# A gated linear-attention and experts kernel: score groups of a head taken by query halves with keys descending, and a new table of places

## What is computed

```python
scores = jnp.einsum('bthd,bshd->bhts', q, k) * scale
logdecay = jnp.where(mask[None, None], Gh[:, :, :, None] - Gh[:, :, None, :], -jnp.inf)
lamw = jnp.einsum('bthl,tsl->bhts', lam, lvl_oh)
A = scores * jnp.exp(logdecay) * lamw
y = jnp.einsum('bhts,bshd->bthd', A, v).reshape(b, t, H * HD)
out = y @ Wo.T + x                      # then a layer norm
...
x = x + _L0_attn_ref(_layernorm(x, axis=-1), ...)
x = x + _L0_ffn_ref(_layernorm(x, axis=-1), ...)
```

## Time and profile before

| | |
|---|---|
| median of 3 runs | 1608.45 us (1607.65 to 1608.62) |
| the profiled execution | 1608.22 us, its span 1606.1 us |
| PE busy | 1456.4 us (91%) |
| POOL busy | 1143.1 us (71%) |
| ACT busy | 1141.3 us (71%) |
| DVE busy | 1030.0 us (64%) |
| granted clock of PE, mean | 0.968 |

### The profile page before, as it was taken

How to read it: one execution, slowest core, us unless ns; L and a number is a source line. 1 busy time by engine, 2 the same in 40 slices (tenths; PEclk the granted TensorE clock), 3 DMA queues, 4 the chain that set the end, 5 groups by cost and what they waited for, 6 DMA issues and landing times.

```text
span 1606.1 us, 29807 instructions
## 1 busy us (share of the span) xinstructions
PE 1456.4 (91%) x10678; PEld 1210.6 (75%) x10678; DVE 1030.0 (64%) x2466; ACT 1141.3 (71%) x3299; POOL 1143.1 (71%) x1067
## 2 busy tenths in 40 slices
PE   5799997899989999899989999899998999989975
PEld 5588886778867887777877788678786887878853
DVE  5457565676657766586655866467674676647665
ACT  2689886786768767686766967678676886867631
POOL 1486779766896678956798667975679666896570
PEclk8799999999999999999999999999999999999987
DMA  5200100010100101001010010001010000100000
GB/s 176 64 18 16 39 28 15 10 37 20 36 15 7 38 22 36 13 15 42 10 35 13 25 36 20 23 16 35 23 36 12 10 26 19 36 16 28 8 8 13
DMA packets 80332, 44.01 MB, mean 27 GB/s; under 512 B 21832, under 2 KB 78522, under 8 KB 80058
## 3 DMA queue, kind: packets, MB, share of 16 engines
q1 hardware_dynamic: 79484, 41.83, 9.2%
q10 hardware_dynamic: 702, 0.29, 0.1%
HBM read 32.39 MB, written 9.18 MB: 26 GB/s over the span
## 4 chain that ended last, share of the span: by engine, by line
PE 55%; POOL 18%; DVE 12%; ACT 9%; issue 4%; DMA 1%; ACTq 0%; SPq 0%; POOLq 0%; DVEq 0%
PE o_ps L1320 15%; PE l_ps L1251 7%; PE s_ps L1235 6%; POOL a_lo L596 6%; PE s_ps L1237 6%; PE s_ps L1236 6%; PE aux L1235 4%; ACT w_all L714 4%; PE aux L1236 4%; PE aux L1237 4%; DVE a_all L912 2%; ACT a_hi L737 2%; POOL ra L581 2%; POOL e_rs L602 1%; POOL yx L441 1%
## 5 line engine op out<-in xcount | busy, mean ns | idle before, releaser
L596 POOL TENSOR_TENSOR a_lo<-a_all,a_hi 128x512 fp32r<-128x512 f32 (+2 forms) x640 | 709.1, 1125 | 323.9 <-ACT a_hi L737 322.7
L912 DVE TENSOR_TENSOR a_all<-s_ps,w_all 128x512 f32<-128x512 f32 (+3 forms) x768 | 422.6, 554 | 488.4 <-PE s_ps L1237 476.3
L714 ACT ACTIVATE w_all<-l_ps,bias 128x128 f32<-128x128 f32 x2304 | 628.5, 386 | 58.1 <-PE l_ps L1251 57.5
L737 ACT ACTIVATE a_hi<-a_all 128x512 fp32r<-128x512 f32 (+2 forms) x640 | 364.0, 591 | 254.8 <-DVE a_all L912 251.5
L1320 PE MATMUL o_ps<-a_hi,v_all 128*128 128x512 f32 (+2 forms) x1280 | 472.1, 373 | 56.9 <-POOL a_lo L596 56.8
L1320 PEld LDWEIGHTS o_ps<-a_hi,v_all 128*128 128x128 f32 x1280 | 243.9, 191 | 110.5 <-POOL a_lo L596 72.5
L1235 PE MATMUL s_ps<-q_hi,xt_hi 128*128 128x512 f32 (+3 forms) x768 | 290.4, 378 | 2.5 <-DVE a_all L912 2.5
L1236 PE MATMUL s_ps<-q_lo,xt_hi 128*128 128x512 f32 (+3 forms) x768 | 268.3, 349 | 0.0
L1237 PE MATMUL s_ps<-q_hi,xt_lo 128*128 128x512 f32 (+3 forms) x768 | 268.0, 349 | 0.0
L1320 PE MATMUL o_ps<-a_lo,v_all 128*128 128x512 f32 (+2 forms) x640 | 232.4, 363 | 0.0
L1237 PEld LDWEIGHTS s_ps<-q_hi,xt_lo 128*128 128x128 f32 x768 | 147.0, 191 | 17.1
...
## 6 DMA issues: line engine op xcount, KB each, us to landing
...
```

The costliest lines, as they stand in the source:

```text
L596: pool.tensor_tensor(a_lo[r][:, 0:t1 - t0], a[r][:, 0:t1 - t0], a_hi[r][:, 0:t1 - t0].bitcast(F32), ALU.subtract).then_inc(a_lo_done, 1)
L714: last = act.activation(w[k][:, W_AT[j] + dd, :].rearrange("p (f c) -> p f c", f=2), l_ps[:, :, slot * HF:(slot + 1) * HF], ACT.Exp, bias= ...
L737: act.activation(a_hi[r][:, 0:t1 - t0], a[r][:, 0:t1 - t0], ACT.Copy).then_inc(a_hi_done, 1)
L912: dve.tensor_tensor(a[(n * NG + g) % NA][:, 0:t1 - t0], s_ps[:, g % 2, 0:t1 - t0], w[n % 2][:, at:at + (t1 - t0) // P, :].rearrange("p i n ...
```

## The change

- GROUPS is ordered anew. First come the queries 0 to 512 with key tiles 3, 2, 1, 0 (widths 128, 256, 384, 512), then the queries 512 to 1024 with key tiles 7 to 0 (128, 256, 384 and five times 512). The FULL groups are now numbers 0 and 4.
- `weigh` waits at each group for the units that this group reads (UNITS_FOR: 1, 2, 3, 4, 1, 2, 3, 4, 5, 5, 5, 5) instead of for all five at group 0. `scores` waits for the second half of q at group 4 instead of at group 1, `values` for each value piece at the first group that reads it, and the value pieces are made in the order of tile pairs 1, 0, 3, 2.
- o_done and y_done become a semaphore for each half of the queries. The first half of o_ps is complete with group 3, the second with group 11. The residual of the second half stands at group 4.
- The tables of places are new. Among the moves: t_apply goes from POOL to ACT (places 56, 58, 64, 80), a quarter of apply2 too (place 101), xb(0) goes ahead of dev1 on POOL, T(0) on PE from place 92 to 104, `total` of the first half from place 273 to 285, the gate step 0 on DVE from place 145 to 144, and the expansions on POOL from places 10 and 21 of a head to 7 and 13.

```diff
--- before.py
+++ after.py
@@ -53,12 +53,8 @@
 
 BIAS_AT = [sum(NC - k for k in range(d)) for d in range(NC)]
 
-GROUPS = []
-for _j in range(NC):
-    for _lo in (0, T // 2):
-        _a = max(_j * P, _lo)
-        if _a < _lo + T // 2:
-            GROUPS.append((_j, _a, _lo + T // 2))
+KEY_ORDER = [(j, f) for f in range(2) for j in reversed(range(NC // 2 * (f + 1)))]
+GROUPS = [(j, max(j * P, f * T // 2), (f + 1) * T // 2) for j, f in KEY_ORDER]
 NG = len(GROUPS)
 
 UNITS = [[(0, 0, 8)], [(1, 1, 7)], [(2, 2, 6)], [(3, 3, 5), (5, 5, 3)], [(4, 4, 4)]]
@@ -151,12 +147,23 @@
 MEAN_VAR = 6
 
 
+V_ORDER = (1, 0, 3, 2)
 LAG = 4
 NA = LAG + 1
 Q_U, NV = 2, 4
 FULL = [g for g, (_j, _a, _b) in enumerate(GROUPS) if _b - _a == P]
 SPLIT = [g for g in range(NG) if g not in FULL]
 FULL_KEYS = [GROUPS[g][0] for g in FULL]
+
+FIRST_OF = [[_a // (T // 2) for _j, _a, _b in GROUPS].index(f) for f in range(2)]
+LAST_OF = [NG - 1 - [_a // (T // 2) for _j, _a, _b in reversed(GROUPS)].index(f) for f in range(2)]
+FIRST_KEYS = {[_j // 2 for _j, _a, _b in GROUPS].index(u): u for u in range(NC // 2)}
+UNIT_OF = {}
+for _u, _parts in enumerate(UNITS):
+    for _d, _i, _n in _parts:
+        for _dd in range(_d, NC if _d == 5 else _d + 1):
+            UNIT_OF[_dd] = _u
+UNITS_FOR = [1 + max(UNIT_OF[i - _j] for i in range(_a // P, _b // P)) for _j, _a, _b in GROUPS]
 
 SLOTS = H * NG
 HALF = T // 2
@@ -169,36 +176,35 @@
 U_AT = {0: 0, 3: 1, 5: 2, 7: 3, 10: 4}
 Q_AT = {6: 0, 20: 1}
 V_AT = {11: 0, 26: 1, 36: 2, 46: 3}
-Q_OUT = {11: 0, 21: 1}
-V_HIGH = {9: 0, 28: 1, 37: 2, 45: 3}
-V_LOW = {18: 0, 32: 1, 41: 2, 49: 3}
-EXPAND_A, EXPAND_B = 10, 21
+Q_OUT = {12: 0, 21: 1}
+V_HIGH = {9: 0, 25: 1, 37: 2, 45: 3}
+V_LOW = {14: 0, 31: 1, 41: 2, 51: 3}
+EXPAND_A, EXPAND_B = 7, 13
...
-             77: [('t_apply', 2)], 81: [('t_apply', 3)], 93: [('dev2', 0)], 96: [('apply2', 0)], 97: [('apply2', 1)],
+ACT_MORE = {12: [('y', 0)], 28: [('y', 1)], 56: [('t_apply', 1)], 58: [('t_apply', 0)], 64: [('t_apply', 2)],
+POOL_MORE = {29: [('xb', 0)], 32: [('dev1', 0)], 33: [('apply1', 0)], 40: [('apply1', 1)], 41: [('t_dev', 0)],
...
         q_hi_done, v_hi_done, v_full_done = sem("q_hi_done"), sem("v_hi_done"), sem("v_full_done")
-        o_done, y_done, ready = sem("o_done"), sem("y_done"), sem("ready")
+        o_done, y_done = ([sem(f"{n}{f}") for f in range(2)] for n in ("o_done", "y_done"))
...
-                    if 2 * u + 1 in FULL_KEYS:
-                        act.activation(v_full[:, r, FULL_KEYS.index(2 * u + 1), :],
+                    j = 2 * V_ORDER[u]
+                    if j + 1 in FULL_KEYS:
+                        act.activation(v_full[:, r, FULL_KEYS.index(j + 1), :],
                                        bank(piece)[:, 2 * P:4 * P].rearrange("p (e n) -> p e n", e=2),
...
@@ -906,8 +916,7 @@
                     at = W_AT[j] + t0 // P - j
                     if n == 0 and g == 0:
                         dve.wait_ge(s_n, 1)
-                    if g == 0:
-                        dve.wait_ge(w_done, (n + 1) * NU)
+                    dve.wait_ge(w_done, n * NU + UNITS_FOR[g])
                     dve.wait_ge(s_mm, n * NG + g + 1)
                     dve.tensor_tensor(a[(n * NG + g) % NA][:, 0:t1 - t0], s_ps[:, g % 2, 0:t1 - t0],
                                       w[n % 2][:, at:at + (t1 - t0) // P, :].rearrange("p i n -> p (i n)"),
@@ -915,11 +924,11 @@
 
                 def take_o(b, f):
 
-                    dve.wait_ge(o_done, 2 * b + f + 1)
+                    dve.wait_ge(o_done[f], b + 1)
                     if b:
                         dve.wait_ge(e["total"], 2 * (b - 1) + f + 1)
                     cols = slice(f * HALF, (f + 1) * HALF)
-                    dve.tensor_tensor(yt[:, cols], o_ps[:, cols], xt_hi[b % 2][:, cols].bitcast(F32), ALU.add).then_inc(y_done, 1)
+                    dve.tensor_tensor(yt[:, cols], o_ps[:, cols], xt_hi[b % 2][:, cols].bitcast(F32), ALU.add).then_inc(y_done[f], 1)
 
                 def statistics(src, stats, i0, s_st):
                     for i in range(i0, i0 + 2):
@@ -1116,8 +1125,10 @@
                             level_logs(b + 1, i)
                         if kind == "l_low" and b + 1 < B:
                             low_logs(b + 1, i)
-                        if kind == "o" and (b or i == 0):
-                            take_o(b - i, i)
+                        if kind == "o" and place >= 2 * NG * H:
+                            take_o(b, i)
+                        if kind == "o" and place < 2 * NG * H and b:
+                            take_o(b - 1, i)
                         if kind == "stat1" and b:
                             first_statistics(b - 1, 2 * i)
                         if kind == "mean1" and b:
@@ -1282,8 +1293,8 @@
                     k, b = n % 2, n // H
                     if n == 0 and g == 0:
                         pe.wait_ge(s_wetc, 2)
-                    if g < Q_U:
-                        wait_taken(pe, ("q", n, g))
+                    if g in FIRST_OF:
+                        wait_taken(pe, ("q", n, FIRST_OF.index(g)))
                     if n or g >= 2:
                         pe.wait_ge(a_done, n * NG + g - 1)
                     keys = slice(j * P, (j + 1) * P)
@@ -1304,11 +1315,10 @@
                     j, t0, t1 = GROUPS[g]
                     b, h = divmod(n, H)
                     r, vr = (n * NG + g) % NA, n % 3
-                    if h == 0 and g < 2:
-                        residual(b, g)
-                    if n % 2 == 0 and g == 0:
-                        for u in range(NV):
-                            wait_taken(pe, ("v", n // 2, u))
+                    if h == 0 and g in FIRST_OF:
+                        residual(b, FIRST_OF.index(g))
+                    if n % 2 == 0 and g in FIRST_KEYS:
+                        wait_taken(pe, ("v", n // 2, V_ORDER.index(FIRST_KEYS[g])))
                     o = o_ps[:, t0:t1]
                     if g in FULL:
                         pe.wait_ge(a_done, n * NG + g + 1)
@@ -1319,8 +1329,8 @@
                         for lhs, rhs in ((v_hi, a_hi), (v_hi, a_lo), (v_lo, a_hi)):
                             last = pe.matmul(o, lhs[:, vr, j, :], rhs[r][:, 0:t1 - t0],
                                              start=False, stop=True, skip_group_check=True)
-                    if h == H - 1 and g in FULL:
-                        last.then_inc(o_done, 1)
+                    if h == H - 1 and g in LAST_OF:
+                        last.then_inc(o_done[LAST_OF.index(g)], 1)
 
                 def claim(piece):
...
```

45 lines of the change are left out of this document (24 added, 21 removed), and 15 rows, old and new, of tables (DVE_MORE, PE_MORE).

## The result

The changed kernel takes 1598.04 us (median of 4 runs, 1596.55 to 1598.31), the kernel before beside it 1608.34 us (1607.65 to 1608.62). The ratio is 0.9935, with a 95% interval of 0.9917 to 0.9952. The change makes the kernel faster by 10.3 us, and not by the 34.5 of the forecast; the time lies 1 us outside the range.

A forecast was written before the change was run, and what follows sets the result against it. PE was taken as the bound, held up by POOL in about one and a half heads a batch. Main term 27.5 plus total 7.0 gave 34.5 us off 1608.22, so 1573.7 (1574 against the median); range 1560 to 1597.

The forecast's parts named there:

- What bounds the kernel: PE is the bound; POOL bounds about one and a half heads a batch, where PE idles 8.0 us.
- The main term: Heads 1 and 2: t_apply and a quarter of apply2 leave POOL, priced one to one at 27.5 us.
- The cap doesn't bind: Heads 1 and 2: the 4.44 us a batch taken off POOL is below PE's 8.0 us of idle time.
- Batch 7 as a trial: Batch 7, heads 1 and 2: POOL busy 5.3 us less, heads 5.7 us shorter, so the stretch follows POOL.
- The rule against ACT: Skill's advice of VectorE for add and mul; rows give it 1 us a batch on ACT; sum left unchanged.
- The group order: New sequence of groups in every head: 0, with bounds of 1.5 us either way for each of 7 batches.
- Gates: Head 3, a unit waiting 2.29 us for exps on ACT: counted 0, bounds 1 us either way a batch.
- total: Head 5: with total later on POOL, the values' 1.00 us wait goes in 7 batches, 7.0 us.
- Finer waits: PE's waits by units, halves and pieces: none of its waits in the rows is of that kind, so 0.
- the two ends: Start and end of the kernel, where the last group becomes 512 wide: counted 0, bounds -1 to +2 us.
- The lower clock: Head 1, PE clock 0.94: fewer gaps could give up to 1.8 us a batch, 1563 us; left out of the sum.
- part comes back: Rival, chance 0.30: POOL meets wide groups when behind, PE waits for a_lo at groups 9 to 11; 1582 to 1600 us.

The follow-up runs named there:

- x14: The changed kernel with level_ln at place 186 instead of 190 and apply1 moved from POOL to DVE at places 41 and 49: 1562.17 us, ratio 0.9702.
- x3: The kernel before with only t_apply and a quarter of apply2 moved from POOL to ACT: 1593.58 us, ratio 0.9905.
- x8: The changed kernel with t_apply and the last quarter of apply2 put back on POOL: 1614.59 us, ratio 1.0033.
- x5: The kernel before with t_apply and a quarter of apply2 on ACT and total of the first half at place 292: 1592.42 us, ratio 0.9896.
- x2: The kernel before, keeping its group order and coarse waits, with the changed kernel's tables of places: 1595.92 us, ratio 0.9921.
- x7: The changed kernel with level_ln on ACT at place 186 instead of 190: 1585.83 us, ratio 0.9850.
- x12: The kernel before, with its old group order and coarse waits, given all the new tables but level_ln at place 186: 1595.22 us, ratio 0.9918.

## Why the prediction was off, step by step

- *What bounds the kernel*: right. PE's waits for a_lo in head 1 were the place to win; x14 took most of them away (0.47 and 0.60 us are left in batch 2) and won 24 us more.
- *The main term*, the step that failed: 27.5 us forecast, 15.4 measured in the old order (x3) and 16.6 in the new (x8). "The cap doesn't bind" was wrong. It compared 4.44 us with all 8.0 us of idle time, but t_apply stands behind the first waits, and behind it there were 3.5 us, of which x3 won 2.8. The bound could be had from PE's timeline and the earlier trace rows: add up the idle time after 462.33. Batch 7 as a trial also misled, since there PE had 3.8 us less to do, which I noted and set aside, and since what POOL hadn't to do there included t_dev, which stands ahead of the waits.
- *The rule against ACT*: ACT took 0.516 us for a t_apply tile and had room; the move is the part that pays. Whether DVE would be better for t_apply wasn't tried; for apply1 DVE was good.
- *The group order*: put at 0 within 10 us. With the old places it costs 24 us, with the new ones between +2 and -9, by one entry of ACT's table. The bounds looked at widths and cover in one head and not at what a place number means once the widths change.
- *Gates and the tables of ACT*: "exp is earlier by 7 places and ln later by 3" spoke of the gates; level_ln, 4 places later, was not priced. This is the omitted step, 12 us: its two table loads had moved past a high_a that waits for DVE.
- *total*: 7.0 forecast, 3.7 measured alone, 1 to 2 in the new order, within the intervals. The named return of a bank's wait came.
- *Finer waits*, *the two ends*: 0, as forecast. From PE's first unit for the last head to the end the two kernels take 91.5 and 91.3 us.
- *The lower clock*: left out of the sum as a possible gain, and it became a small loss: in three of the seven batches head 1 stands at 0.88 and is 1.0 us longer than where it stands at 0.94 (last section). "I take batch 2 for all" hid that head 1 differed before too, from 1.00 in batch 1 to 0.89 in batches 5 and 6.
- *The rivals*: the range of "part comes back", 1582 to 1600, holds the result, and it had one part of the mechanism, PE's waits for a_lo. It put them at groups 9 to 11. One is there (group 11 of head 0, 0.79 us), but 3.9 us are at groups 1 and 2 of head 1. ACT's waits came too, at head 4, from level_ln and not from t_apply.

In a sum, from runs: in the old order the move and total give 16.9 us (x5). The whole set of tables gives 13.1 in that order (x2), so the other entries cost 4. The new order adds 9 to 11 us to what they give if level_ln is at 186 (x7, x12), and takes 3 away, within the intervals, if it is at 190. By batches, batch 0 is 4.1 us longer than before, 0.8 of it by level_ln. Of the rest 1.4 us lie in head 2 (22.0 us for 20.6), which x2 has too (22.2), so they come with the tables; by which entry is open.
